# A transformer layer on one core: order of the mixing stage, late score units, and the engine of the feed-forward norm

## The reference

```python
def reference(x, w_qkv, b_qkv, w_out, b_out, W1, W2, W3):      # x: 4 x 512 x 256, all float32
    qkv = layernorm(x) @ w_qkv.T + b_qkv                       # 16 heads of 16
    q, k, v = heads(qkv);  q, k = rope(q), rope(k)
    p = softmax(causal(q @ k.T / 4))
    x = x + layernorm((p @ v) @ w_out.T + b_out)
    n = layernorm(x)                                           # the feed-forward norm
    hidden = fwht(silu(n @ W1.T) * (n @ W3.T))                 # 1024 wide, Walsh-Hadamard
    return x + layernorm(hidden @ W2.T)
```

## Time and profile before

| | |
|---|---|
| median of 3 runs | 500.91 us (500.86 to 501.76) |
| profiled execution | 497.78 us, span 496.1 us |
| granted clock of PE, mean | 0.938 |
| busy share of the span | PE 82%, PEld 68%, DVE 57%, ACT 43%, POOL 33% |
| chain that ended last | PE 58%, DVE 13%, DMA 9%, issue 7%, ACT 6% |

### The profile page before, as it was taken

The page is one execution under the profiler, slowest core; times in us unless marked ns, Lnnn a source line. Parts: engine busy times, 40 slices in busy tenths (PEclk is TensorE's granted clock), DMA queues, the critical chain, the costliest instruction groups (busy, mean ns, idle before and its releaser), DMA issues.

```text
span 496.1 us, 7892 instructions
## 1 busy us (share of the span) xinstructions
PE 405.0 (82%) x2884; PEld 338.2 (68%) x2884; DVE 281.2 (57%) x936; ACT 210.9 (43%) x314; POOL 162.1 (33%) x284
## 2 busy tenths in 40 slices
PE   1679677999599997988599988987799979858992
PEld 1569645558489985557499975566699965448991
DVE  7554583625937776536856776267576754273114
ACT  4445234753323337843423347813332367423221
POOL 4136002533512226514422235614132245321232
PEclk9999865999969999999889999999799999997998
DMA  6549900000397000200695001102880002000001
GB/s 230 215 136 247 212 1 1 2 2 0 127 255 171 1 1 1 85 1 1 179 245 130 1 1 42 44 1 72 219 201 21 1 1 85 1 1 1 1 1 42
DMA packets 35463, 36.95 MB, mean 74 GB/s; under 512 B 2016, under 2 KB 34528, under 8 KB 35424
## 3 DMA queue, kind: packets, MB, share of 16 engines
q1 hardware_dynamic: 35424, 36.45, 26.6%
HBM read 21.76 MB, written 14.68 MB: 73 GB/s over the span
## 4 chain that ended last, share of the span: by engine, by line
PE 58%; DVE 13%; DMA 9%; issue 7%; ACT 6%; SPq 3%; POOL 2%; DVEq 0%; POOLq 0%; ACTq 0%
PE ps L266 30%; PE ps L448 8%; PE ps L464 7%; PE ps L436 5%; DMA qk_scratch<-qk_s 4%; DMA q_t<-qk_scratch 4%; ACT probs L656 4%; DVE masked_scores L923 2%; SPq L293 2%; DMA raw_bias<-in_b_out 2%; PE ps L498 2%; DVE xy L985 1%; POOL hid_s L803 1%; PE ps L405 1%; DVE stats_h L870 1%
## 5 line engine op out<-in xcount | busy, mean ns | idle before, releaser
L923 DVE CUSTOM_DVE_ANT_0 masked_scores<-ps,mask_row 128x128 bf16<-128x128 f32 (+3 forms) x256 | 114.4, 488 | 61.6 <-PE ps L436 61.1
L266 PE MATMUL ps<-xt,w_s 128*128 128x256 f32 x768 | 111.7, 294 | 0.0
L266 PEld LDWEIGHTS ps<-xt,w_s 128*128 128x128 f32 x768 | 106.2, 202 | 0.5
L803 POOL TENSOR_TENSOR hid_s<-gate,hid_s 128x512 fp32r<-128x512 f32 x32 | 41.2, 1287 | 135.9 <-ACT hid_s L668 135.9
L656 ACT ACTIVATE probs<-ps 128x1280 f32<-128x1280 f32 x64 | 76.4, 1242 | 9.5 <-PE ps L448 8.9
L436 PE MATMUL ps<-k_t,q_t 96*128 96x128 f32 (+3 forms) x256 | 71.7, 356 | 9.8 <-DMA q_t<-qk_scratch 5.6
L448 PEld LDWEIGHTS ps<-q_t,k_t 128*128 128x128 f32 x256 | 44.9, 198 | 32.2 <-ACT probs L656 14.7
L266 PE MATMUL ps<-w_s,hid_s 128*128 128x256 f32 x384 | 55.5, 284 | 7.0 <-POOL hid_s L803 7.0
L448 PE MATMUL ps<-q_t,k_t 128*128 128x512 f32 (+3 forms) x256 | 55.7, 345 | 5.6 <-ACT probs L656 4.0
L266 PEld LDWEIGHTS ps<-w_s,hid_s 128*128 128x128 f32 x384 | 51.6, 190 | 9.3 <-POOL hid_s L803 8.7
L436 PEld LDWEIGHTS ps<-k_t,q_t 96*128 96x128 f32 x256 | 43.0, 198 | 18.6 <-DVE maxima L923 10.9
(11 more groups left out here) (99 smaller groups left out, 485.3 us busy)
## 6 DMA issues: line engine op xcount, KB each, us to landing
qk_scratch<-qk_s SPq DMA_DIRECT2D x32, 256.0 KB, 5.6
k_t<-qk_scratch SPq DMA_DIRECT2D x16, 384.0 KB, 5.5
q_t<-qk_scratch SPq DMA_DIRECT2D x8, 768.0 KB, 8.8
qk_scratch<-qk_s SPq DMA_DIRECT2D x8, 512.0 KB, 5.5
xa<-in_x SPq DMA_DIRECT2D x4, 512.0 KB, 9.6
xy<-in_x SPq DMA_DIRECT2D x4, 512.0 KB, 3.5
out<-xy SPq DMA_DIRECT2D x8, 256.0 KB, 2.3
o_t<-in_w SPq DMA_DIRECT2D x1, 1024.0 KB, 10.0
```

The costliest lines, as they stand in the source:

```text
L266: ins = eng.matmul(o, lhs(i), rhs(j), start=first and n == 0, stop=last and n == 2, skip_group_check=skip)
L803: pool.tensor_tensor(hid_s[:, a % 2, 1, :], gate[:, a % 2, :], hid_s[:, a % 2, 0, :].bitcast(F32), ALU.subtract).then_inc(S["hid_l"], 1)
L923: ins = dve.tensor_tensor_reduce(masked_scores[:, SCORE_NO[n] % 2, i * keys:(i + 1) * keys], ps[:, banks[n], i * keys:(i + 1) * keys], mas ...
```

## The change

Five edits, one of which is only an order: (1) `MIX`: step y3 stands ahead of q1 instead of behind r0; r1 stands behind w0; N0, N1, H0, H1, u0, u1 run before r2, and r3 comes after u3; (2) the feed-forward norm N moves from DVE to ACT, for which POOL negates the shift (one more instruction for each half); `MIX_LAST` gets the same split in halves; (3) exp's table is loaded behind the last silu instead of the last `hid_high`; (4) `UNITS_AFTER` puts all 42 units into the slices, with no unit left behind the last downs; (5) the last turn's transpose follows head 8 instead of 7, ACT and POOL handle list entry 5 behind head 7 (before: ahead of head 6) and entry 6 behind head 8, and the first `values` waits for one score unit less.

```diff
@@ -72,7 +72,8 @@
 TAIL_BANKS = [6 + n % 2 for n in range(TAIL)] + [7]
-TAIL_AFTER = {4: (0, 2), 5: (2, 4), 6: (4, 6), 7: (6, 7)}
+TAIL_AFTER = {4: (0, 2), 5: (2, 4), 6: (4, 6), 8: (6, 7)}
+TAIL_COPY_AFTER = {7: 5, 8: 6}
...
 def turn_of(unit):

@@ -95,12 +96,11 @@
-MIX = """o0 o1 d0 d1 n0 n1 q0 l0 l1 e0 c0 o2 d2 y0 o3 s0 n2 y1 l2 d3 s1 n3 y2 v0 l3 q1 r0 y3 s2 s3 e1 c1 t0
-    v1 e2 c2 q2 R0 r1 R1 w0 R2 R3 t1 q3 w1 r2 e3 c3 N0 N1 N2 t2 r3 N3 t3 H0 L0 H1 L1 H2 L2 H3 L3 u0 u1
-    u2 u3""".split()
+MIX = """o0 o1 d0 d1 n0 n1 q0 l0 l1 e0 c0 o2 d2 y0 o3 s0 n2 y1 l2 d3 s1 n3 y2 v0 l3 y3 q1 r0 s2 s3 e1 c1 v1 t0
+    q2 R0 R1 w0 r1 R2 R3 w1 t1 q3 e2 c2 N0 N1 H0 L0 H1 L1 u0 u1 r2 N2 N3 t2 e3 c3 H2 L2 H3 L3 u2 u3 r3 t3""".split()
 FIRST_MIX = "e0 c0 q0 e1 c1 q1 r0 q2 t0 r1 e2 c2 q3 t1 e3 c3 r2 t2 r3 t3".split()
-MIX_LAST = """o0 o1 d0 d1 n0 n1 l0 l1 o2 d2 y0 s0 n2 o3 y1 l2 d3 s1 n3 y2 v0 l3 y3 s2 s3 v1 R0 R1 w0 R2 R3 w1 N0
-    N1 N2 N3 H0 L0 H1 L1 H2 L2 H3 L3 u0 u1 u2 u3""".split()
+MIX_LAST = """o0 o1 d0 d1 n0 n1 l0 l1 o2 d2 y0 s0 n2 o3 y1 l2 d3 s1 n3 y2 v0 l3 y3 s2 s3 v1 R0 R1 w0 R2 R3 w1
+    N0 N1 H0 L0 H1 L1 u0 u1 N2 N3 H2 L2 H3 L3 u2 u3""".split()
...
 def feed_forward_steps(units_after):

@@ -139,7 +139,7 @@
-UNITS_AFTER = [(0, 0, 0), (3, 2, 0), (2, 3, 0), (4, 1, 0), (4, 2, 0), (4, 3, 0), (4, 3, 0), (4, 1, 0), (0, 0, 1)]
+UNITS_AFTER = [(0, 0, 0), (3, 2, 0), (2, 3, 0), (4, 1, 0), (4, 2, 0), (4, 4, 0), (4, 4, 0), (4, 0, 0), (0, 0, 1)]
...
 UNIT_BANKS = unit_banks(EARLY_UNITS)

@@ -453,7 +453,7 @@
                     if g == 0:
-                        pe.wait_ge(S["maxed"], (b + 1) * N_SCORES)
+                        pe.wait_ge(S["maxed"], (b + 1) * N_SCORES - 1)
...
                         pe.wait_ge(S["rows_in"], 2 * (b + 1) * N_TURNS)

@@ -564,6 +564,8 @@
                     pe.wait_ge(S["hid_l"], b * HCH + a + 1)
+                if a == 0 and t == 2 and b < BATCHES - 1:
+                    pe.wait_ge(S["qk_l"], (b + 2) * TILES)
...
                              a == 0 and t % 2 == 0, a == HCH - 1 and t % 2 == 1, skip=True)

@@ -697,8 +699,12 @@
                         high(b, t, "turned_n", two(ps[:, N_BANK[t], 0:DIM]), xt2[:, 0, :, t * P:t * P + P], "on_h")
-                    elif m == "N0":
-                        act.activation(spare[:, :], minus_half[:, 0:1], ACT.Silu)
+                    elif m[0] == "N":
+                        if t == 0:
+                            act.activation(spare[:, :], minus_half[:, 0:1], ACT.Silu)
+                        act.wait_ge(S["ln_h%d" % (t // 2)], 2 * b + 2)
+                        act.activation(y[:, t, :], xr[:, t, :], ACT.Identity, scale=rstd["h"][:, t:t + 1],
+                                       bias=shift["h"][:, t:t + 1]).then_inc(S["norm_h"], 1)
...
                     elif m == "u3":

@@ -708,10 +714,10 @@
                         silu(b, n)
+                        if n == HCH - 1:
+                            act.activation(spare[:, :], minus_half[:, 0:1], ACT.Exp)
...
                         hid_high(b, n)
-                        if n == HCH - 1:
-                            act.activation(spare[:, :], minus_half[:, 0:1], ACT.Exp)
...

@@ -755,8 +761,8 @@
                     exps(b, h)
-                    for n in range(*TAIL_AFTER.get(h + 1, (0, 0))):
-                        score_unit(b, TAIL_UNITS[n], UNIT_BANKS if b else FIRST_UNIT_BANKS)
+                    if h in TAIL_COPY_AFTER:
+                        score_unit(b, TAIL_UNITS[TAIL_COPY_AFTER[h]], UNIT_BANKS if b else FIRST_UNIT_BANKS)
...
                         xt_high(b + 1, t)

@@ -781,6 +787,9 @@
                     .then_inc(S["ln_" + which], 1)
+                if which[0] == "h":
+                    pool.wait_ge(S["ln_" + which], 2 * b + 1)
+                    pool.tensor_scalar(s, s, -1.0, None, ALU.mult).then_inc(S["ln_" + which], 1)
...
                     pool.tensor_tensor(s, s, shift["y"][:, tiles], ALU.add).then_inc(S["ln_" + which], 1)

@@ -826,8 +835,8 @@
                     cut(b, h)
-                    for n in range(*TAIL_AFTER.get(h + 1, (0, 0))):
-                        max_low(b, TAIL_UNITS[n])
+                    if h in TAIL_COPY_AFTER:
+                        max_low(b, TAIL_UNITS[TAIL_COPY_AFTER[h]])
...
                 for m in order:

@@ -987,10 +996,6 @@
                             tile_stats("h%d" % (t // 2), t - 1, xr[:, t - 1, :])
-                    elif m[0] == "N":
-                        dve.wait_ge(S["ln_h%d" % (t // 2)], b + 1)
-                        dve.tensor_scalar(y[:, t, :], xr[:, t, :], rstd["h"][:, t:t + 1], shift["h"][:, t:t + 1],
-                                          ALU.mult, ALU.subtract).then_inc(S["norm_h"], 1)
...

```

## The result

The changed kernel takes **533.66 us** (median of 4 runs, 531.61 to 534.99) beside 500.88 us for the kernel before (498.36 to 501.76). The ratio is 1.066, with a 95% interval of 1.0608 to 1.0711: slower by 33 us, 30 to 36. The forecast was 521, its range ended at 527. The direction was right and the size was not.

What follows compares the result with a forecast made beforehand. PE was taken to bound the kernel, busy 82% of the span. Edit 5 7.5, edits 3 and 4 6.4, mixing 4.2 and clock 2 sum to 20 us, on 500.9: 521 us, range 512 to 527.

Steps and rivals of the forecast that it cites:

- values one maximum earlier: Attention, last turn: the first values wait for one maximum less, 0.6 us of DVE's work, so start about 198.4 instead of 199.03.
- `max_low` behind root and two cuts: Attention, last turn: POOL's queue delays PE's transpose and next values by 1.6, 2.65, 2.65 and 0.6 us, 7.5 in all.
- the single waits: Feed-forward, last slices: PE waits 0.7 us for a maximum, 0.55 for ACT's copies, 0.3 in the slice before.
- the term of 0.65: Last pass, edit 3: without units, the table load lengthens the chain to the last downs by 0.65 us.
- unit 0 bound by the fetch: Mixing: q's fetch is issued 1.55 us later, making unit 0 later by 0, 1.4 and 1.5 us in three passes.
- If the products between the transposes run at 0.50 ... it is up to 7.4: Mixing, edits 1 and 2: at half clock between the transposes the cost is up to 7.4 us instead of 4.2.
- the gain ends in front of the fetch: Mixing: PE reaches u0 about 3 us earlier, later waits cost about 1 us each, and unit 0 still waits for q's fetch.
- as much or more: Mixing, rival (d): PE waits 1.58 us before r1 and at least that before three later steps, some 6.7 us; chance 0.03.
- It may happen in none or both, 0 to 3.4: Attention, second and third pass: half clock behind the new 3.3 us stall; 2 us taken, including mixing's doubtful part.
- The 3.4 us that the forecast had there: Attention behind the new stall: some 3.4 us of dense work at half clock take 1.7 us longer.
- Rival (b): The clock falls in every stall: 500.9 + 18.1 + 3.4 + 3.2 = 526 us; chance 0.2.
- The drain that the Trainium skill adds to each table load: ACT's table loads: about 1.4 us more each, some 5.5 us in sum; left out because the trace does not bear it out.

Runs made afterwards that it cites:

- k4_turn_root: Edit 5 alone on the kernel before, with the root of x on POOL moved behind head 8's cut and `max_low`; 499.60 us, ratio 0.9984 to 1.0031.
- the added products: Changed kernel plus matmuls that change no output, in PE's waits ahead of the last turn (three passes) and in mixing (every pass); 526.89 us, ratio 1.0499 to 1.0578.
- k2_units_table: Edits 3 and 4 alone on the kernel before; 505.75 us, ratio 1.0081 to 1.0187.
- k6_mixing_fill: Edits 1 and 2 alone on the kernel before, plus matmuls that change no output in PE's mixing waits; 503.89 us, ratio 1.0064 to 1.0140.
- k7_table: Edit 3 alone on the kernel before, exp's table loaded ahead of the last `hid_high`; 504.48 us, ratio 1.0080 to 1.0150.

## Why the prediction was right and where it failed

**Edit 5, right in its waits.** Each step holds: values one maximum earlier, `max_low` behind root and two cuts, 1.6, 2.65, 2.65 and 0.6. With the clock held the stages show 2.19, 2.67, 2.67 and 0.50, 8.0 against 7.5, and k4_turn_root shows that the place behind the root makes the cost. One reading was wrong without harm: PE does not wait once in the attention of the second pass but five times, 2.6 us in all, four of them at its start.

**Edits 3 and 4, near in their sum, in part by luck.** They cost 6.7 us (4.0 to 9.3) against 6.4, and the single waits are as said. But edit 3 alone cost 5.7 against 2.3 and edit 4 alone 5.4 against 4.1, and in the last pass the term of 0.65 measured 1.92 in one execution. Why both together cost less than the sum is not shown.

**Edits 1 and 2, the sum near, the mechanism not the one at work.** The forecast had 4.2 with unit 0 bound by the fetch. With PE kept busy the part costs 5.1 (3.2 to 7.0) and the fetch binds. In the changed kernel itself it does not: unit 0 waits for nothing, and is late by 3.65, 4.29 and 4.58 us where 0, 1.4 and 1.5 were forecast. "If the products between the transposes run at 0.50 ... it is up to 7.4" named the case that came, and priced it 5 us too low (12.2 measured). The step that fell is "the gain ends in front of the fetch": in the three passes of the changed kernel PE comes to unit 0 2.7 to 3.6 us after the fetch has landed. The reading that PE waits "as much or more" before each of three later steps was also wrong (1.54, 2.62 and 0.98 us in the first pass), while their sum of 6.7 with r1's 1.58 is right.

**The clock, the step that failed.** "It may happen in none or both, 0 to 3.4; with the doubtful part of the mixing stage I take 2 us." Measured on the parts, with and without PE kept busy, it is 5.2 us in attention (12.9 less 7.7) and 7.1 in mixing (12.2 less 5.1), 12.3 in all. In the whole kernel the added products give back 6 us by the ratios and 12 between the profiled executions, so what it costs there is not known better than that. Two things were sized wrong. In attention it fell in three passes, behind the wait of 2.06 us too, and in the second pass it held for 5.9 us of work, a cost of 2.3 us. The 3.4 us that the forecast had there, at a cost of 1.7, came from no row. And in mixing it was not asked what the products cost that stand between several short waits: 2.93 for 1.70 us, twice, then 2.28 and 1.05 for 1.67 and 0.60. By the parts, what is left with PE kept busy (7.7, 6.7 and 5.1) is 19.5, forecast 18.1, and the clock is 12.3 in the place of 2: 31.8 for 20, nearly the whole miss. The split is not clean, since the clock also falls for a time in k2_units_table and in k6_mixing_fill, so that the 19.5 us hold some of it. Rival (b) had the right mechanism, and with 6.6 us for it still too little.

The Trainium skill (TensorE: Matmul & The Clock Gate, What's actually happening) has idleness throttle the array and activity release it. The rows agree: 3.11 us idle and the scores behind take 1.44 instead of 0.86 us, 14 products in the place of the idle time and they take 0.86. The drain that the Trainium skill adds to each table load (ScalarE: Activation LUTs, What ACT_TABLE_LOAD costs) was rightly left out: in k7_table the load starts 0.01 us behind the silu and the next ACTIVATE 1.30 us behind the load's start (183.44 and 184.74), so no drain shows.
